# Moving a gamma scaling, a row part and the last beta additions in a fused attention and mixture kernel

## What is computed

```python
x = x + attn(layernorm(x), Wqkv, bqkv, Wo, bo)          # one head of 256
x = x + ffn(layernorm(x), gate_w, up_w, down_w, fc1_w, fc2_w, expert_w, ln_gamma, ln_beta)

def ffn(h, ...):
    logits  = h @ gate_w                                 # 8 experts
    weights = top_k(logits, 2)
    shared  = relu(h @ up_w) ** 2 @ down_w               # 1024 -> 2048 -> 1024
    routed  = ((h @ fc1_w) @ expert_w * sum(weights)) @ fc2_w
    return layernorm(shared + routed) * ln_gamma + ln_beta
```

## Time and profile before

| what | value |
|---|---|
| time, median of 3 runs | 2261.93 us (2258.81 to 2262.75) |
| time of the profiled execution | 2259.66 us |
| its span, from first to last record | 2257.9 us |
| outside of the span | 1.76 us |
| mean granted clock of the tensor engine | 0.997 of full speed |
| PE busy | 2213.0 us, 98% of the span |
| DVE busy | 1479.9 us, 66% |
| ACT busy | 610.0 us, 27% |
| Pool busy | 543.6 us, 24% |
| moved by DMA | 502.75 MB |

### The profile page before, as it was taken

One profiled execution on the slowest core, in us unless ns is written; L12 is line 12 of the kernel. 1 busy time (PEld: TensorE's weight loads), 2 busy tenths in 40 slices (PEclk: granted clock), 3 DMA queues, 4 the chain that ended last, 5 costly groups with the idle time before them and its releaser, 6 DMA issues.

```text
span 2257.9 us, 36554 instructions
## 1 busy us (share of the span) xinstructions
PE 2213.0 (98%) x15001; PEld 1423.4 (63%) x15001; DVE 1479.9 (66%) x1851; ACT 610.0 (27%) x950; POOL 543.6 (24%) x464
## 2 busy tenths in 40 slices
PE   6999999999999999999999999999999999999998
PEld 5656556666665444585487478468558648846853
DVE  7766478788985899775565466376466546637615
ACT  4333334335322664232022012112202201211200
POOL 2332000000002689352043023114204203311400
PEclk9999999999999999999999999999999999999999
DMA  9988289999897888879668777956967886795672
GB/s 230 234 180 189 66 177 225 251 240 225 185 218 206 258 309 286 275 239 282 206 215 233 240 228 208 307 188 202 283 201 218 244 235 223 208 306 173 202 227 85
DMA packets 510951, 502.75 MB, mean 223 GB/s; under 512 B 330816, under 2 KB 351424, under 8 KB 510784
## 3 DMA queue, kind: packets, MB, share of 16 engines
q1 hardware_dynamic: 501040, 470.00, 74.2%
q10 hardware_dynamic: 8880, 27.27, 4.1%
q0 software_dynamic: 864, 3.15, 0.3%
HBM read 351.44 MB, written 69.73 MB: 187 GB/s over the span
## 4 chain that ended last, share of the span: by engine, by line
PE 89%; DVE 4%; DMA 2%; issue 2%; SPq 1%; ACT 1%; POOL 1%; ACTq 0%; POOLq 0%; DVEq 0%
PE psum L97 63%; PE psum L2084 22%; PE psum L2031 3%; DMA arena<-arena 1%; POOL arena L324 1%; DVE arena L1294 1%; DVE arena L1278 1%; DMA arena<-in_attn_Wqkv 0%; DVE arena L510 0%; SPq L286 0%; DMA x<-arena 0%; ACT arena L841 0%; DMA arena<-in_ffn_ln_beta 0%; PE psum L1996 0%; DVE arena L1818 0%
## 5 line engine op out<-in xcount | busy, mean ns | idle before, releaser
L97 PE MATMUL psum<-arena 128*128 128x256 f16 (+1 forms) x11592 | 1602.4, 301 | 13.9 <-DVE arena L1818 3.3
L97 PEld LDWEIGHTS psum<-arena 128*128 128x128 f16 x11592 | 1133.7, 98 | 478.0 <-issue 11.3
L2084 PE MATMUL psum<-arena 128*128 128x512 f16 x2352 | 509.9, 379 | 0.0
L2084 PEld LDWEIGHTS psum<-arena 128*128 128x128 f16 x2352 | 230.1, 98 | 276.0
L1532 POOL TENSOR_TENSOR arena<-arena 128x256 f32<-128x256 f32 x70 | 95.5, 1364 | 435.4 <-ACT arena L1658 435.4
L841 ACT ACTIVATE arena<-psum,b_nb,consts 128x512 f32<-128x512 f32 x128 | 97.9, 774 | 198.2 <-DVE b_nb L960 198.2
L1801 DVE TENSOR_TENSOR arena<-arena 128x1536 f16<-128x1536 f32 (+1 forms) x28 | 59.0, 2108 | 123.8 <-ACT arena L1582 122.9
L1587 ACT ACTIVATE c_ystd<-c_ymv,c_epsc,consts 128x1 f32<-128x1 f32 x32 | 12.4, 387 | 412.6 <-DVE c_ymv L1823 412.6
L1519 POOL TENSOR_TENSOR arena<-arena 128x256 f32<-128x256 f32 x56 | 41.8, 746 | 283.4 <-DVE arena L1911 283.4
L1641 ACT ACTIVATE arena<-arena 128x768 f16<-128x768 f32 x56 | 47.2, 843 | 230.0 <-DVE arena L1911 230.0
L1645 ACT ACTIVATE arena<-arena 128x1024 f16<-128x1024 f32 x56 | 59.2, 1057 | 174.1 <-POOL arena L1525 174.1
(11 more groups left out here) (160 smaller groups left out, 1795.5 us busy)
## 6 DMA issues: line engine op xcount, KB each, us to landing
arena<-ws_in SPq DMA_DIRECT2D x210, 512.0 KB, 3.8
arena<-ws_out SPq DMA_DIRECT2D x196, 512.0 KB, 4.8
arena<-in_attn_x SPq DMA_DIRECT2D x64, 512.0 KB, 4.9
arena<-x SPq DMA_DIRECT2D x64, 512.0 KB, 6.5
arena<-ws_in SPq DMA_DIRECT2D x70, 256.0 KB, 3.6
x<-arena SPq DMA_DIRECT2D x32, 512.0 KB, 3.7
out<-arena SPq DMA_DIRECT2D x32, 512.0 KB, 6.2
ws_in<-arena SPq DMA_DIRECT2D x30, 512.0 KB, 4.4
```

The costliest lines, as they stand in the source:

```text
L97: last = nc.tensor.matmul(out, lhs(a, c), rhs(b, c), start=(c == 0 and n == 0), stop=(c == chunks - 1 and n == len(PRODUCTS) - 1))
L2084: mm = nc.tensor.matmul(product_banks(m)[:, u, :], rS[:, c, a, LEFT[m], u * P:(u + 1) * P], w2[slot_of(i, n)][:, cc, b, :], start=(c == 0 ...
```

## The change

It has three parts. None changes what is computed, apart from the order in which beta and the residual are added in two output tiles.

1. **Gamma.** The wait for the loads of gamma and beta and the scaling of gamma leave DVE's opening. They stand now in `first_body`, in the turn p = 4, behind the splits of that pair.
2. **The last row part.** On DVE the low part of row part 3 of block 1 moves from ahead of `routed(0)` to behind its first output tile, ahead of the other three.
3. **Beta.** In the last block, Pool adds beta to the residual rows of output tiles 2 and 3 (a new semaphore, `xres_summed`). On DVE, L1830 and L1832 become one instruction there: the row times the reciprocal plus that sum. For the last tile it is issued in two halves of 512 columns, and SP stores each half by a DMA of its own.

```diff
@@ mixture, semaphores and constants
+    xres_summed = sem("xres_summed")
-    PARTS_AT, STATS_AT, DIFFERENCES_AT = (UP + 1, 13, 16, 17), 14, (13, 16)
+    PARTS_AT, STATS_AT, DIFFERENCES_AT, GAMMA_AT = (UP + 1, 13, 16, 17), 14, (13, 16), 4
@@ sync_program
-        for t in range(2, TILES):
-            store(NBLK - 1, t)
-        for t in range(TILES):
-            hold(out_sent[t], 16 * (NBLK + 1))
+        store(NBLK - 1, 2)
+        t = r_order(NBLK - 1)[TILES - 1]
+        for h, cols in enumerate((cols2, cols1)):
+            hold(out_ready, TILES * NBLK + 2 + h)
+            sync.dma_start(out_d[NBLK - 1, t][:, cols], acc[:, t, cols]).then_inc(out_sent[t], 16)
+        for n in range(TILES):
+            hold(out_sent[n], 16 * (NBLK + 1 + (n == t)))
@@ pool_program, body
+                return
+            pool.wait_ge(gb_in, 32)
+            for q in range(R_EARLY, TILES):
+                pool.wait_ge(xres_in[q % 2], 16 * (2 * i + q // 2 + 1))
+                pool.tensor_tensor(xres[q % 2], xres[q % 2], beta, ALU.add).then_inc(xres_summed, 1)
@@ dve_program, opening
-        dve.wait_ge(gb_in, 32)
-
-        steps.link(dve.tensor_scalar(gamma, gamma, consts[:, C_SHARED:C_SHARED + 1], None, ALU.mult))
@@ dve_program, routed
                 steps.link(dve.reciprocal(yrstd[:], ystd[:]))
+                if last and q >= R_EARLY:
+
+                    dve.wait_ge(xres_summed, q - R_EARLY + 1)
+                    for cols in (cols2, cols1) if q == TILES - 1 else (slice(0, H),):
+                        dve.scalar_tensor_tensor(row[:, cols], row[:, cols], yrstd[:], xres[q % 2][:, cols], ALU.mult, ALU.add
+                                                 ).then_inc(out_ready, 1)
+                    continue
                 steps.link(dve.scalar_tensor_tensor(row, row, yrstd[:], beta, ALU.mult, ALU.add))
@@ dve_program, first_body
+                if p == GAMMA_AT:
+                    dve.wait_ge(gb_in, 32)
+                    steps.link(dve.tensor_scalar(gamma, gamma, consts[:, C_SHARED:C_SHARED + 1], None, ALU.mult))
@@
-                if p in PARTS_AT:
+                if p in PARTS_AT[:3]:
                     next_part(0, PARTS_AT.index(p))
@@
-            routed(0, False)
+            routed(0, False, range(1))
+            next_part(0, 3)
+            routed(0, False, range(1, TILES))
```

More of the change, by code:

```diff
@@ L1832, in routed @@
                 dve.tensor_tensor(row, row, xres[q % 2], ALU.add).then_inc(out_ready, 1)
-            assert steps.n == OUT * len(tiles)
+            assert steps.n == OUT * len(tiles) - len([q for q in tiles if last and q >= R_EARLY])
         def first_body():
```

## The result

The changed kernel takes 2249.74 us (median of 13 runs, 2246.08 to 2255.52) against 2261.72 us for the kernel before (13 runs, 2256.44 to 2265.76). The ratio is 0.9948, with a 95% interval from 0.9936 to 0.9960, so it is about 12 us or 0.5% faster.

The account below looks back on a forecast made before the run. With PE busy 98% of the span, only its stalls, lower clock and the tail could be won: 3.2 + 3.1 + 1.8 + 2.9 = 11.0 us, from the median 2261.93 to 2250.9, range 2247.5 to 2257.0.

Parts of the forecast that it names:

- Part 1, direct: Block 0's opening: moving gamma's scaling removes PE's waits of 2.5 and 0.7 us; 3.2 us, bounds 2.0 and 3.2.
- The wait for L1605: Ahead of the down products: PE's 0.7 us wait for ACT's drain of the last latent product goes too.
- DVE up to 7.9 us ahead: From the split for tile 4 in block 0, DVE's stream runs up to 7.1 + 0.8 = 7.9 us earlier.
- (a): Block 0's tail, paced by the pair stream, gives the opening's gain back: 3.2 lost, 2254.1; chance 0.12.
- (b): End of block 0: Pool's pair sums of turn 17 meet output tile 0; 4.9 lost, 2255.8; chance 0.10.
- Part 2, the step that failed: Ahead of block 1: moving the row part behind output tile 0 removes nearly all of PE's 3.3 us stall; 3.1 us.
- In the new order, counted on the same clock: End of block 0: tile 0 done at 923.2, row part 925.5, tile 2's second sum 934.9, as late as the gate product.
- The clock: Block 1's first 9.17 us: the lower granted clock (mean 0.81) goes with the stall ahead of it; 1.8 us.
- Part 3: Kernel's tail: one DVE instruction less for tiles 2 and 3, last tile in halves; 2.9 us, bounds 1.4 and 3.1.
- the half store: Kernel's end: the last DMA, half as large, gains between 0 and 0.7 us; taken as 0.5.
- (c): Tail: tile 3's residual lands late and L1827 waits behind Pool's sum; likely 1.3 us lost, 2252.2; chance 0.08.
- (d): Behind output tile 0, the row part holds the gate product back; 6.3 us slower than before, 2268.2; chance 0.03.

Follow-up runs that it names:

- part 1 alone: Only the scaling of gamma moved to turn 4, against the kernel before; row part and tail as before: ratio 0.9972 (0.9957 to 0.9986), 6.3 us faster.
- part 2 alone: Only the low part of row part 3 moved behind output tile 0, against the kernel before; gamma and tail as before: ratio 1.0007 (0.9992 to 1.0022).

## Why the prediction was right, and where it was not

- **The size.** 2250.9 was forecast and 2249.74 measured; the sum was 11.0, the trace shows 11.4.
- **Part 1, direct.** 3.2 forecast, 3.53 in the stretch. The two waits were 3.18 us long; the other 0.35 went with the two stops. DVE's first split of tile 4 began 19.64 us behind PE's start in the mixture (741.82 - 722.18), held only by the attention's stores; forecast 735.8 - 716.5 = 19.3. The wait for L1605 is gone too, as forecast.

```profile
741.82 2.48 DVE L1279 SCALAR_TENSOR_TENSOR arena<-arena,scales 128x1024 f16<-128x1024 f32 x2 [10.80 <-DMA x<-arena]
```

- **DVE up to 7.9 us ahead.** Measured against the mixture's start, the first split came 7.6 us earlier (27.23 us before, 19.64 after), and the low part of row part 2 at the end of block 0 came 6.7 us earlier (193.73 us before, 187.03 after). Of these, 3.5 are PE's own gain, so that 3.2 are a real lead over PE. The prediction had the 7.9 us and used them only to argue that moved work is hidden and that (a) and (b) are unlikely. It did not carry them to the next stall.
- **Part 2, the step that failed.** "In the new order, counted on the same clock" left DVE's and Pool's position against PE as it was before. With that, 3.1 us for the stall and 1.8 for the clock fell to the row part. The runs give them to gamma: part 1 alone leaves a stall of 0.3 us and no low clock, part 2 alone leaves 1.9 us and the low clock. The total came out right because both edits work on one stall, and it can be removed but once: 3.21 and 1.67 us in the stretches. That part is luck: by the same working the move alone would have been forecast at 4.9 us, and it gave 1.4 by the stretches (1.34 and 0.06), while gamma alone would have been forecast at 3.2 and gave 8.2.
- **The clock.** 1.8 forecast, 1.67 found. It came back with the stall.
- **Part 3.** 2.9 forecast, 3.00 found. DVE gained what the rows said (the step of tile 3 from 2.55 to 1.42 us); the half store was put at 0.5 and brought 0.6 (landing 2.0 instead of 2.6 us behind its issue), or 0.48 net of the 0.14 us that the second instruction costs DVE. Pool's 1024 columns take 2.36 us, estimated 2.5; its distance from L1833 is 0.37 us, forecast 0.3.
- **The rivals.** (b) and (c) didn't happen but exist, each shown by a run. (b) was priced at 4.9 us; the two runs in which it came true lost 3.0 and 3.5 us against the changed kernel in the second and third columns. (d) exists too, from 2.3 us of further delay on. (a) was wrong at its root: the pair stream did come earlier.

What stays open: the row part's own worth, 0.25 to 0.8 us, is from two single traces, too small for the totals. That the stall is removed by part 1 rests on single traces too, one for each kernel; but the six kernels that have gamma moved and the row part no later than behind tile 0 have 0 to 0.8 us of stall there, and the four with gamma at the opening have 1.4 to 3.3.

## What to carry to other kernels

When an edit lets a stream start earlier, carry the lead to every later place where that stream is last, before a second edit is credited with the same stall. And compare stretches by their own starts where the executions differ ahead of them. An idle engine that is handed work can block its neighbour: look at what runs in the window in which its operation will land, not only at whether it is ready in time.

## What the runs showed of the hardware

The cost of a stall of the tensor engine is not its length alone. Ahead of block 1, behind the small gate matmuls, stalls of 1.4, 1.9, 3.1 and 3.3 us were each followed by a granted clock at the lower level (1.2 GHz) for part of the next 9.17 us (0.68 to 0.82 in the mean), which took 1.6 to 2.8 us of further time by the third column; stalls of 0.3 and 0.8 us were not. A stall of 4.7 us ahead of the gate matmuls cost 2.0 us in the same way. At the opening, behind a run of large matmuls, 2.4 and 2.5 us left the clock at 1.00, and 3.0 us brought it to 0.81, which cost 1.7 us. These are single executions, and what decides between them was not tried.

A DVE operation with two inputs in SBUF and a Pool sum take turns: in four cases in two runs the DVE operation ended 1.08 or 1.09 us behind the end of the Pool sum that it met, whether that sum was 512 or 1024 columns wide.
